# A macaron block on one core: the heads' products in 64-row, 64-column pieces, plain W_v products in the second FFNs, and another order of small steps

## The chip, the cores and the metric

The kernel runs on one core of a Trainium2 chip. The engines of the core work side by side and wait for each other by semaphores: TensorE (PE; its weight loads are shown as PEld), VectorE (DVE), ScalarE (ACT), GpSimd (POOL) and SyncE (SP), which issues most DMAs. The metric is device time in microseconds (us) from start to end of one execution.

## What is computed

The reference, cut to what matters. x has 4096 tokens (2 sequences of 2048) of 256 features; all arithmetic is 32-bit.

```python
def ffn(x):                       # 2 sequences of 2048 tokens, C = 256
    x_prev = x shifted by one token, zeros first
    xr = mu_r * x + (1 - mu_r) * x_prev
    xk = mu_k * x + (1 - mu_k) * x_prev
    r = sigmoid(xr @ W_r.T)
    k_act = square(relu(xk @ W_k.T))
    return r * (k_act @ W_v.T)

def attn(x):                      # 16 heads of 16 features
    q = relu(x @ Wq.T) / 4;  k = relu(x @ Wk.T) / 4
    v = x @ Wv.T;            u = silu(x @ Wu.T)
    kv = einsum('bhlk,bhlv->bhkv', k, v)
    out = einsum('bhlk,bhkv->bhlv', q, kv)
    return (srms_norm(out) * u) @ Wo.T      # norm over the 16 features of a head

x = x + 0.5 * ffn(layernorm(x))
x = x + attn(layernorm(x))
x = x + 0.5 * ffn(layernorm(x))
```

## The kernel before

The tokens are cut into 8 blocks of 512 (NB = 8), each of 4 tiles of 128 tokens. `xs` holds all of x in SBUF from start to end. The program runs through 16 iterations n: n = 0 to 7 are the first FFN of blocks 0 to 7, n = 8 to 15 the second FFN of blocks 0 to 7. Beside the first FFN of block i stand the attention's projections of block i-1 (k, u, q, and the Gram product of x and k, from which kv follows once a sequence is complete), and beside the second FFNs the last steps of the attention of blocks j = n-5. Every engine's stream is written out by hand in program order; nothing is scheduled by a planner. Between the FFN iterations 7 and 8 lies a stretch that has no FFN product, only attention work (blocks 6 and 7).

Most products are "split": the 32-bit operands a and b are cut into a high part, which ACT makes by rounding to the fp32r format, and a low part, the rest, which POOL or DVE makes by subtraction; the product is then three fp32r products, hi*hi, hi*lo and lo*hi (`product`, L1076 to L1079). Other products are "plain": one matmul of 32-bit operands, which the compiler makes into two passes, so that it has two records in the trace. The transposes have one record each.

The steps that the change and the prediction name:

- `attend(j)` (PE, L1234): the heads' outputs of block j. q of the block lies with features on partitions; `kv_bd` is a 128 x 128 matrix for each half of the features, block-diagonal with eight 16 x 16 blocks. For each of 4 token tiles and 2 feature halves one plain product of 128 rows and 128 columns, 16 records a call, 8 calls. They go into two PSUM banks (`psA` for j < 4, `psK` after), tokens of tiles 0 and 1 into the first, 2 and 3 into the second.
- `square_heads` (ACT), `gate_heads` (DVE, L886: times `silu_u`), `head_norms` (DVE, L892 to L921: sum of squares of each head, then a reciprocal root in a chain of 64-element operations, then the first half of gout), `norm_second` (POOL, L265: the second half of gout), `transpose_g` (PE, L1247), `project_out` (PE: split product with Wo), `add_attention` (DVE, L931).
- `ffn_k`, `ffn_r` (PE, split products with W_k and W_r), `transpose_a` (PE, L1094: transposes the normalized block), `previous`, `mix_high` and `normalize` (ACT), `mix_current` (DVE, L806), `k_low` (POOL, L359) and `r_low` (POOL L366 or DVE): they make the mixed inputs of the next FFN and their high and low parts.
- `ffn_v` (PE, split product with W_v, 24 records) and `ffn_v2` (PE, L1146, plain product with W_v, 16 records). The second FFNs n = 8 to 11 use the first, n = 12 to 15 the second: `SPLIT2 = 12` says where it changes. The split one needs `act_hi` (ACT, L565) and `act_lo` (`act_low2`, POOL, L416) beside the square itself (L567).
- `scales_a(n)` (POOL: four small operations on the statistics of `stats_a(n)`, DVE, for the layernorm of FFN n), `scales_b(a)` and `stats_b(a)` (the same for the attention), `add_ffn2(n)` (POOL, L424: adds a second FFN's result to xs, after which SP stores the block), `x1_low`, `kt_low` (POOL, L395 and L404: low parts for the Gram product), `keep_g` (DVE, L871).

Each engine works in its own written order, so a step that waits holds up all that is written behind it on that engine.

## Time and profile before

| | us |
|---|---|
| median of 3 runs | 323.66 (323.63 to 323.96) |
| profiled execution | 323.19 |
| its span, first to last instruction | 321.5 |
| PE busy | 309.6, 96% of the span |
| PE weight loads busy | 280.2, 87% |
| DVE busy | 239.8, 75% |
| ACT busy | 239.7, 75% |
| POOL busy | 215.0, 67% |

An engine's busy time says how full it is. PE's products are pipelined: each record is longer than the distance from its start to the next one's, so a block's price is read from the start of its first record to the start of what follows. The inputs and weights have arrived before a fourth of the span is over; the stores of the second FFNs' blocks run beside the last iterations.

### The profile page before, as it was taken

The page shows a single profiled execution, that of the slowest core. Times are in us where ns is not written, and L with a number is a line of the kernel's source. Part 1 is how long each engine was busy: PE and PEld are TensorE (multiplying, and loading weights), DVE is VectorE, ACT ScalarE, POOL GpSimd, SP SyncE. Part 2 cuts the span into 40 slices and gives each one's busy share as a digit, 9 for nine tenths or more (in the row PEclk, how much of TensorE's full clock was granted, in tenths as well). Part 3 has the DMA queues.
Part 4 walks back from the last instruction along what each step waited for, and adds up shares of the span by engine and source line. Part 5 has one row for each costly group of instructions (what it writes and reads, how often), then busy time and mean ns, then how long its engine had stood idle before and what let it go on. Part 6 is the DMA issues. An engine that isn't in the chain of part 4 may idle for free.

```text
span 321.5 us, 5807 instructions
## 1 busy us (share of the span) xinstructions
PE 309.6 (96%) x2052; PEld 280.2 (87%) x2052; DVE 239.8 (75%) x566; ACT 239.7 (75%) x465; POOL 215.0 (67%) x234
## 2 busy tenths in 40 slices
PE   6898999999999999999999999999999999998996
PEld 6677898899889988988988998889998989887985
DVE  3689984595675746895894797686989988995744
ACT  3698967969869679679259367479797979679861
POOL 4297858769778578669358217536687979797560
PEclk9999999999999999999999999999999999999999
DMA  7960000000000000000000000000002020121103
GB/s 215 352 219 0 3 1 0 2 0 2 0 1 3 0 2 0 0 2 0 2 2 0 2 0 2 0 3 1 2 1 67 0 67 0 66 67 66 65 2 131
DMA packets 11036, 10.85 MB, mean 34 GB/s; under 512 B 768, under 2 KB 11008, under 8 KB 11008
## 3 DMA queue, kind: packets, MB, share of 16 engines
q1 hardware_dynamic: 10432, 10.23, 9.8%
q8 instruction: 16, 0.26, 0.3%
q10 hardware_dynamic: 576, 0.26, 0.3%
q14 instruction: 12, 0.10, 0.1%
HBM read 6.29 MB, written 4.19 MB: 33 GB/s over the span
## 4 chain that ended last, share of the span: by engine, by line
PE 68%; DVE 15%; POOL 7%; issue 5%; ACT 4%; DMA 1%; SPq 0%; POOLq 0%; ACTq 0%
PE psK L1077 7%; PE psK L1078 7%; PE psK L1079 7%; PE psRV L1077 6%; PE psRV L1079 6%; PE psRV L1078 6%; PE psX L1078 6%; PE psX L1077 6%; PE psX L1079 6%; PE psK L1234 2%; PE psA L1094 2%; PE psX L1161 2%; PE psRV L1146 2%; DVE head_ss L892 1%; POOL gout L265 1%
## 5 line engine op out<-in xcount | busy, mean ns | idle before, releaser
L806 DVE SCALAR_TENSOR_TENSOR mix<-psA,mu,mix 128x512 f32<-128x512 f32 x64 | 44.0, 741 | 11.1 <-ACT mix L525 11.1
L359 POOL TENSOR_TENSOR mix_k_lo<-mix,mix_k_hi 128x512 fp32r<-128x512 f32 x30 | 39.2, 1328 | 12.9 <-ACT mix_k_hi L543 12.8
L525 ACT ACTIVATE mix<-psA,one_mu 128x511 f32<-128x511 f32 x64 | 39.5, 696 | 2.2 <-PE psA L1094 2.2
L512 ACT ACTIVATE xn<-xs,shiftA,rstdA 128x256 f32<-128x256 f32 x59 | 30.8, 603 | 12.4 <-POOL shiftA L343 12.4
L1077 PE MATMUL psRV<-ffn_hi,mix_r_hi 128*128 128x256 f32 x128 | 36.4, 284 | 0.0
L1079 PE MATMUL psRV<-ffn_hi,mix_r_lo 128*128 128x256 f32 x128 | 35.8, 279 | 0.0
L1078 PE MATMUL psRV<-ffn_lo,mix_r_hi 128*128 128x256 f32 x128 | 35.7, 279 | 0.0
L1077 PE MATMUL psK<-mix_k_hi,ffn_hi 128*128 128x512 f32 x64 | 26.1, 408 | 1.8 <-DVE mix_k_lo L961 1.5
L1077 PE MATMUL psRV<-ffn_hi,act_hi 128*128 128x256 f32 x96 | 27.5, 287 | 0.0
L1079 PE MATMUL psRV<-ffn_hi,act_lo 128*128 128x256 f32 x96 | 26.8, 279 | 0.0
L1078 PE MATMUL psRV<-ffn_lo,act_hi 128*128 128x256 f32 x96 | 26.8, 279 | 0.0
L1078 PE MATMUL psK<-mix_k_lo,ffn_hi 128*128 128x512 f32 x64 | 25.3, 395 | 0.0
L1079 PE MATMUL psK<-mix_k_hi,ffn_lo 128*128 128x512 f32 x64 | 25.3, 395 | 0.0
L404 POOL TENSOR_TENSOR k_lo<-k_tok,k_hi 128x512 fp32r<-128x512 f32 x14 | 18.1, 1293 | 10.3 <-ACT k_hi L590 10.3
L778 DVE BATCH_NORM_STATS2 statsA<-xs 128x6 f32<-128x256 f32 x64 | 22.6, 412 | 2.7 <-DMA xs<-x_dram 2.4
L1078 PEld LDWEIGHTS psRV<-ffn_lo,mix_r_hi 128*128 128x128 f32 x128 | 24.1, 188 | 0.4
L1077 PEld LDWEIGHTS psRV<-ffn_hi,mix_r_hi 128*128 128x128 f32 x128 | 24.0, 188 | 0.4
L1079 PEld LDWEIGHTS psRV<-ffn_hi,mix_r_lo 128*128 128x128 f32 x128 | 24.0, 188 | 0.0
L543 ACT ACTIVATE mix_k_hi<-mix 128x512 fp32r<-128x512 f32 x32 | 19.9, 653 | 3.5 <-DVE mix L806 3.5
L844 DVE TENSOR_TENSOR x_lo<-psX,x_hi 128x512 fp32r<-128x512 f32 x16 | 10.3, 683 | 14.8 <-ACT x_hi L580 14.7
L333 POOL TENSOR_SCALAR var_epsA<-meanvarA 128x4 f32<-128x4 f32 x16 | 4.7, 294 | 23.7 <-DVE meanvarA L786 22.7
L395 POOL TENSOR_TENSOR x_lo<-xs,x_hi 128x512 fp32r<-128x512 f32 x14 | 17.9, 1302 | 3.5 <-ACT x_hi L585 3.5
(157 smaller groups left out, 1066.3 us busy)
## 6 DMA issues: line engine op xcount, KB each, us to landing
xs<-x_dram SPq DMA_DIRECT2D x7, 512.0 KB, 8.7
out_dram<-xs SPq DMA_DIRECT2D x7, 512.0 KB, 2.9
out_dram<-xs SPq DMA_DIRECT2D x4, 128.0 KB, 1.7
xs<-x_dram ACTq DMA_DIRECT2D x2, 128.0 KB, 2.9
xs<-x_dram SPq DMA_DIRECT2D x2, 128.0 KB, 2.6
silu_u<-w_ffn_k_dram SPq DMA_DIRECT2D x1, 256.0 KB, 5.0
q_store<-w_k_dram SPq DMA_DIRECT2D x1, 256.0 KB, 5.2
silu_u<-w_ffn_r_dram SPq DMA_DIRECT2D x1, 256.0 KB, 6.5
```

The lines of the kernel that those rows point to most:

```text
L359: nc.gpsimd.tensor_tensor(mix_k_lo[:, h, :], mix[:, 0, h, :], mix_k_hi[:, h, :].bitcast(F32), ALU.subtract).then_inc(s_lo_k, 1)
L395: nc.gpsimd.tensor_tensor(x1_lo[:, g * BANK:(g + 1) * BANK], row(xs, a, g * BANK, BANK), x1_hi[:, g * BANK:(g + 1) * BANK].bitcast(F32), A ...
L404: nc.gpsimd.tensor_tensor(k_lo[:, tiles, :], k_tok[:, tiles, :], k_hi[:, tiles, :].bitcast(F32), ALU.subtract).then_inc(s_kt_lo, 1)
L512: nc.scalar.activation(xn[:, t, :], tile_row(xs, b, t), ACT.Identity, bias=shiftA[:, t:t + 1], scale=rstdA[:, t:t + 1]).then_inc(s_xn, 1)
L525: nc.scalar.activation(mix[:, rk, h, 1:BLOCK], psA[:, h, 0:BLOCK - 1], ACT.Copy, scale=one_mu[:, rk, h:h + 1]).then_inc(s_prev, 1)
L543: nc.scalar.activation(hi[:, h, :], mix[:, rk, h, :], ACT.Identity).then_inc(done, 1)
L778: nc.vector.bn_stats(statsA[:, t, :], tile_row(xs, b, t)).then_inc(s_bnA, 1)
L806: nc.vector.scalar_tensor_tensor(out=m, in0=psA[:, h, :], scalar=mu[:, rk, h:h + 1], in1=m, op0=ALU.mult, op1=ALU.add).then_inc(s_mix, 1)
L844: nc.vector.tensor_tensor(x2_lo[:, h, :], psX[:, h, :], x2_hi[:, h, :].bitcast(F32), ALU.subtract).then_inc(s_x2lo, 1)
L1077: nc.tensor.matmul(dst, a_hi, b_hi, start=start, stop=False)
L1078: nc.tensor.matmul(dst, a_hi, b_lo, start=False, stop=False)
L1079: return nc.tensor.matmul(dst, a_lo, b_hi, start=False, stop=stop)
```

## The change

Three things are changed.

1. `attend`: each 128 x 128 product becomes two of 64 rows and 64 columns, for the two 64 x 64 blocks on the diagonal of `kv_bd`; what lies outside them is zero. The products of rows 0 to 63 go into the first PSUM bank and those of rows 64 to 127 into the second, alternating. A bank now holds 64-column pieces of all four token tiles. `gate_heads` and the sum in `head_norms` read the banks in such pieces, and the signals of both banks come with the last two products.
2. W_v of all second FFNs is plain: `ffn_v2` in n = 8 to 11 too. `act_low2` and the ACT operation for `act_hi` are gone there.
3. Order. DVE: `add_attention(0)` and `add_attention(1)` stand ahead of `stats_b(6)` and `stats_b(7)`; `stats_a(9)` stands behind `mix_current(8)`. POOL: `x1_low(7)`, `norm_second(2)`, `kt_low(7)` stand ahead of `scales_a(9)`; from n = 12 on, `add_ffn2(n-1)` stands at the end of the iteration and no longer ahead of `scales_a` and `k_low`.

```diff
+QUAD = 4 * HEAD
-        SPLIT2 = 12
+        def by_quad(ap, g):
+            return ap.rearrange("p (q g e) -> p q g e", g=2, e=QUAD)[:, :, g, :]
...
@@ pool
-            scales_a(9)
-            norm_second(2)
-            x1_low(7)
-            kt_low(7)
+            x1_low(7)
+            norm_second(2)
+            kt_low(7)
+            scales_a(9)
             k_low(8)
             scales_a(10)
             for n in range(8, LAST):
-                if n < SPLIT2:
-                    norm_second(n - 5)
-                    act_low2(n)
-                    if n > 8:
-                        scales_a(n + 2)
-                    k_low(n + 1)
-                    r_low(n + 1)
-                    if n > 8:
-                        add_ffn2(n - 1)
-                else:
-                    if n - 5 < NB:
-                        norm_second(n - 5)
-                    add_ffn2(n - 1)
-                    if n + 2 <= LAST:
-                        scales_a(n + 2)
-                    k_low(n + 1)
-                    if n == 12:
-                        r_low(n + 1)
+                if n - 5 < NB:
+                    norm_second(n - 5)
+                if n > 8 and n + 2 <= LAST:
+                    scales_a(n + 2)
+                k_low(n + 1)
+                if n < 13:
+                    r_low(n + 1)
+                if n > 8:
+                    add_ffn2(n - 1)
             add_ffn2(14)
@@ activate_k2, act
-                        act.wait_ge(s_act_lo, 2 * min(n, SPLIT2))
+                        act.wait_ge(s_act_lo, 2 * NB)
...
-                    if n < SPLIT2:
-                        nc.scalar.activation(act_hi[:, h, :], act_k[:, h, :], ACT.Square).then_inc(s_act_hi, 1)
-                        act.wait_ge(s_act_hi, 2 * n + h + 1)
@@ gate_heads, head_norms, dve
-                    nc.vector.tensor_tensor(gout[:, 2 * g:2 * g + 2, :].rearrange("p t d -> p (t d)"), ps[:, g, :],
-                                            row(silu_u, j % HELD, g * BANK, BANK), ALU.mult).then_inc(s_gu, 1)
+                    nc.vector.tensor_tensor(by_quad(gout[:].rearrange("p t d -> p (t d)"), g),
+                                            ps[:, g, :].rearrange("p (q e) -> p q e", e=QUAD),
+                                            by_quad(row(silu_u, j % HELD), g), ALU.mult).then_inc(s_gu, 1)
...
-                    nc.vector.tensor_reduce(head_ss[:, g * n:(g + 1) * n], by_head(squares[:, g, :]),
+                    nc.vector.tensor_reduce(head_ss[:].rearrange("p (q g k) -> p q g k", g=2, k=4)[:, :, g, :],
+                                            squares[:, g, :].rearrange("p (q k e) -> p q k e", k=4, e=HEAD),
@@ attend, pe
                 for t in range(TILES):
                     for h in range(HALVES):
-                        last = nc.tensor.matmul(ps[:, t // 2, (t % 2) * D + h * P:(t % 2) * D + (h + 1) * P],
-                                                q_half(j, h)[:, tok(t)], kv_bd[:, j // BB, h, :],
-                                                start=True, stop=True)
-                    if t % 2:
-                        last.then_inc(s_o, 1)
+                        for g in range(2):
+                            part = slice(g * QUAD, (g + 1) * QUAD)
+                            col = (t * HALVES + h) * QUAD
+                            last = nc.tensor.matmul(ps[:, g, col:col + QUAD], q_half(j, h)[part, tok(t)],
+                                                    kv_bd[part, j // BB, h, part], start=True, stop=True)
+                            if t == TILES - 1 and h == HALVES - 1:
+                                last.then_inc(s_o, 1)
@@ the second FFNs, pe
                 if n < 12:
                     attend(j + 1, [(s_relu, 2 * (n + 1))])
-                    ffn_v(n)
-                    project_out(j)
-                else:
-                    ffn_v2(n)
-                    project_out(j)
+                ffn_v2(n)
+                project_out(j)
```

DVE's stream between iterations 7 and 8, before, from x2_low(7) to the first silu of block 7 (x_lo<-psX is x2_low(7), statsA and meanvarA are stats_a(9), g_acc is keep_g(6), mix is mix_current(8)):

```order
L844 TENSOR_TENSOR x_lo<-psX,x_hi 128x512 [waits s_x2hi] x2
L778 BN_STATS statsA<-xs 128x6 [waits s_x2,s_aggA]
L778 BN_STATS statsA<-xs 128x6 x3
L786 BN_AGGR meanvarA<-statsA 128x2 [waits s_bnA,s_lnA]
L786 BN_AGGR meanvarA<-statsA 128x2 [waits s_bnA] x3
L871 TENSOR_TENSOR g_acc<-g_acc,psK 128x512 [waits s_gacc,s_gt]
L806 SCALAR_TENSOR_TENSOR mix<-psA,mu,mix 128x512 [waits s_prev] x4
L811 TENSOR_TENSOR halo<-one_mu,psA 128x4
L850 SCALAR_TENSOR_TENSOR silu_u<-psX,rstdB,silu_u 128x256 [waits s_sig] x2
```

And after the change:

```order
L829 TENSOR_TENSOR x_lo<-psX,x_hi 128x512 [waits s_x2hi] x2
L856 TENSOR_TENSOR g_acc<-g_acc,psK 128x512 [waits s_gacc,s_gt]
L791 SCALAR_TENSOR_TENSOR mix<-psA,mu,mix 128x512 [waits s_prev] x4
L796 TENSOR_TENSOR halo<-one_mu,psA 128x4
L763 BN_STATS statsA<-xs 128x6 [waits s_x2,s_aggA]
L763 BN_STATS statsA<-xs 128x6 x3
L771 BN_AGGR meanvarA<-statsA 128x2 [waits s_bnA,s_lnA]
L771 BN_AGGR meanvarA<-statsA 128x2 [waits s_bnA] x3
L835 SCALAR_TENSOR_TENSOR silu_u<-psX,rstdB,silu_u 128x256 [waits s_sig] x2
```

The two rows of statistics and the two of aggregates now follow the four mixes and the halo column.

POOL's stream at the same place, before, from scales_b(7) to k_low(8) (var_epsA to shiftA are scales_a(9), gout is norm_second(2), x_lo<-xs is x1_low(7), k_lo is kt_low(7)):

```order
L352 TENSOR_TENSOR rstd2B<-rstdB 128x4 [waits s_lnB]
L333 TENSOR_SCALAR var_epsA<-meanvarA 128x4 [waits s_aggA]
L339 TENSOR_TENSOR rstdA<-var_epsA,minus_half 128x4 [waits s_xn,s_mvA]
L341 TENSOR_TENSOR mean_rstdA<-meanvarA,rstdA 128x4 [waits s_lnA]
L343 TENSOR_SCALAR shiftA<-mean_rstdA 128x4 [waits s_lnA]
L265 TENSOR_TENSOR gout<-gout,head_rn 128x512 [waits s_gu,s_rn]
L395 TENSOR_TENSOR x_lo<-xs,x_hi 128x512 [waits s_x1hi] x2
L404 TENSOR_TENSOR k_lo<-k_tok,k_hi 128x512 [waits s_kt_hi] x2
L359 TENSOR_TENSOR mix_k_lo<-mix,mix_k_hi 128x512 [waits s_hi_k] x2
```

And after:

```order
L356 TENSOR_TENSOR rstd2B<-rstdB 128x4 [waits s_lnB]
L399 TENSOR_TENSOR x_lo<-xs,x_hi 128x512 [waits s_x1hi] x2
L269 TENSOR_TENSOR gout<-gout,head_rn 128x512 [waits s_gu,s_rn]
L408 TENSOR_TENSOR k_lo<-k_tok,k_hi 128x512 [waits s_kt_hi] x2
L337 TENSOR_SCALAR var_epsA<-meanvarA 128x4 [waits s_aggA]
L343 TENSOR_TENSOR rstdA<-var_epsA,minus_half 128x4 [waits s_xn,s_mvA]
L345 TENSOR_TENSOR mean_rstdA<-meanvarA,rstdA 128x4 [waits s_lnA]
L347 TENSOR_SCALAR shiftA<-mean_rstdA 128x4 [waits s_lnA]
L363 TENSOR_TENSOR mix_k_lo<-mix,mix_k_hi 128x512 [waits s_hi_k] x2
```

scales_a(9), which waits for the aggregates of stats_a(9), went from the head of this piece to behind kt_low(7).

POOL's stream in iterations 12 and 13, before, from norm_second(7) to the add of block 4 (xs<-xs,k_tok is add_ffn2(11), then come scales_a(14), k_low(13), r_low(13), and xs<-xs,gate is add_ffn2(12)):

```order
L265 TENSOR_TENSOR gout<-gout,head_rn 128x512 [waits s_gu,s_rn]
L424 TENSOR_TENSOR xs<-xs,k_tok 128x512 [waits s_gated] x2
L333 TENSOR_SCALAR var_epsA<-meanvarA 128x4 [waits s_aggA]
L339 TENSOR_TENSOR rstdA<-var_epsA,minus_half 128x4 [waits s_xn,s_mvA]
L341 TENSOR_TENSOR mean_rstdA<-meanvarA,rstdA 128x4 [waits s_lnA]
L343 TENSOR_SCALAR shiftA<-mean_rstdA 128x4 [waits s_lnA]
L359 TENSOR_TENSOR mix_k_lo<-mix,mix_k_hi 128x512 [waits s_hi_k] x2
L366 TENSOR_TENSOR mix_r_lo<-mix,mix_r_hi 128x512 [waits s_hi_r] x2
L424 TENSOR_TENSOR xs<-xs,gate 128x512 [waits s_gated] x2
```

And after:

```order
L269 TENSOR_TENSOR gout<-gout,head_rn 128x512 [waits s_gu,s_rn]
L337 TENSOR_SCALAR var_epsA<-meanvarA 128x4 [waits s_aggA]
L343 TENSOR_TENSOR rstdA<-var_epsA,minus_half 128x4 [waits s_xn,s_mvA]
L345 TENSOR_TENSOR mean_rstdA<-meanvarA,rstdA 128x4 [waits s_lnA]
L347 TENSOR_SCALAR shiftA<-mean_rstdA 128x4 [waits s_lnA]
L363 TENSOR_TENSOR mix_k_lo<-mix,mix_k_hi 128x512 [waits s_hi_k] x2
L370 TENSOR_TENSOR mix_r_lo<-mix,mix_r_hi 128x512 [waits s_hi_r] x2
L421 TENSOR_TENSOR xs<-xs,k_tok 128x512 [waits s_gated] x2
```

The add of iteration 11 went behind r_low(13); add_ffn2(12), not shown any more, moved behind k_low(14) in the same way.

## Rows read from the trace of the kernel before

**Rows 1.** The page: busy time, share and instructions of each engine; TensorE's granted clock.

```profile
PE 309.6 (96%) x2052; PEld 280.2 (87%) x2052; DVE 239.8 (75%) x566; ACT 239.7 (75%) x465; POOL 215.0 (67%) x234
...
PEclk9999999999999999999999999999999999999999
```

**Rows 2.** Waits of TensorE: who waited <- for whom: total us, times, longest us.

```profile
PE psRV L1146 <- ACT k_tok L573: 1.1, 1, 1.1
PE psK L1077 <- POOL k_lo L404: 0.7, 1, 0.7
```

**Rows 3.** Timeline of PE in iteration 8: start, length, line, shapes [idle before].

```profile
219.28 1.95 PE L1234 MATMUL psK<-kv_bd,q_store 128*128 128x128 f32 x16
220.98 0.37 PE L1077 MATMUL psRV<-ffn_hi,act_hi 128*128 128x256 f32 x1
...
223.90 0.28 PE L1077 MATMUL psX<-wo_hi,g_hi 128*128 128x256 f32 x1
```

**Rows 4.** Timeline of PE: the plain W_v product of iteration 13 and what follows.

```profile
295.29 3.69 PE L1146 MATMUL psRV<-ffn_v_plain,act_k 128*128 128x256 f32 x16 [1.07 <-ACT k_tok L573]
298.81 1.04 PE L1094 MATMUL psA<-ident,xn 128*128 128x128 f32 x8
```

**Rows 5.** Timeline of PE's weight loads (PEld) behind the wait at 203 us.

```profile
203.12 0.19 PEld L1077 LDWEIGHTS psK<-k_hi,x_hi 128*128 128x128 f32 x1 [0.87 <-POOL k_lo L404]
203.23 0.19 PEld L1078 LDWEIGHTS psK<-k_lo,x_hi 128*128 128x128 f32 x1
```

**Rows 6.** Timeline of PE's products at the same place.

```profile
203.13 0.39 PE L1077 MATMUL psK<-k_hi,x_hi 128*128 128x256 f32 x1 [0.67 <-POOL k_lo L404]
203.35 0.28 PE L1078 MATMUL psK<-k_lo,x_hi 128*128 128x256 f32 x1
```

**Rows 7.** Line 1234, the heads' products: ns shortest/median/longest, first and last start.

```profile
L1234 PE MATMUL psK<-kv_bd,q_store x64: 274/275/276, 219.3 to 267.0; 128*128 128x128 f32 x64
```

**Rows 8.** Timeline of DVE: head_norms in iteration 9 (229) and 10 (243).

```profile
229.09 0.20 DVE L908 TENSOR_SCALAR head_y<-head_ss 128x64 int32<-128x64 int32 x1
...
243.65 0.85 DVE L905 SCALAR_TENSOR_TENSOR head_ss<-var_epsB,head_ss 128x64 f32<-128x64 f32 x1
244.53 1.19 DVE L908 TENSOR_SCALAR head_y<-head_ss 128x64 int32<-128x64 int32 x1
```

**Rows 9.** Timeline of POOL at that time.

```profile
243.14 2.53 POOL L424 TENSOR_TENSOR xs<-xs,gate 128x512 f32<-128x512 f32 x2
```

**Rows 10.** Timeline of PE: both transposes of iterations 10 (247) and 12 (278).

```profile
247.17 1.04 PE L1094 MATMUL psA<-ident,xn 128*128 128x128 f32 x8
248.42 0.63 PE L1247 MATMUL psX<-ident,gout 128*128 128x128 f32 x4 [0.21 <-DVE gout L265]
249.25 0.66 PE L1247 MATMUL psX<-ident,gout 128*128 128x128 f32 x4 [0.20 <-POOL gout L265]
...
278.65 1.03 PE L1094 MATMUL psA<-ident,xn 128*128 128x128 f32 x8
279.53 0.60 PE L1247 MATMUL psX<-ident,gout 128*128 128x128 f32 x4
280.32 0.66 PE L1247 MATMUL psX<-ident,gout 128*128 128x128 f32 x4 [0.20 <-POOL gout L265]
```

**Rows 11.** Timeline of POOL, iterations 12 and 13: the add of block 3 and r_low(13).

```profile
280.23 2.50 POOL L424 TENSOR_TENSOR xs<-xs,k_tok 128x512 f32<-128x512 f32 x2
...
287.24 2.52 POOL L366 TENSOR_TENSOR mix_r_lo<-mix,mix_r_hi 128x512 fp32r<-128x512 f32 x2
```

**Rows 12.** Timeline of ACT there: mix_high(13, 0), second half, and previous(14).

```profile
284.12 0.63 ACT L543 ACTIVATE mix_k_hi<-mix 128x512 fp32r<-128x512 f32 x1 [0.57 <-DVE mix L806]
...
289.84 0.21 ACT L519 ACTIVATE mix<-halo 128x4 f32<-128x4 f32 x1 [2.08 <-issue]
```

**Rows 13.** Timeline of DVE between iterations 7 and 8: stats_a(9) and keep_g(6).

```profile
192.87 1.39 DVE L778 BATCH_NORM_STATS2 statsA<-xs 128x6 f32<-128x256 f32 x4
...
194.47 0.65 DVE L871 TENSOR_TENSOR g_acc<-g_acc,psK 128x512 f32<-128x512 f32 x1
```

More of the change, by code:

```diff
@@ L410, in norm_second @@
                 norm_half(nc.gpsimd, 1).then_inc(s_gn1, 1)
-            def act_low2(n):
-                for h in range(HALVES):
-                    pool.wait_ge(s_act, 2 * (n - NB) + h + 1)
-                    nc.gpsimd.tensor_tensor(act_lo[:, h, :], act_k[:, h, :], act_hi[:, h, :].bitcast(F32),
-                                            ALU.subtract).then_inc(s_act_lo, 1)
             def add_ffn2(n):
@@ L885, in gate_heads @@
                         dve.wait_ge(s_tg, 2 * j)
-                    nc.vector.tensor_tensor(gout[:, 2 * g:2 * g + 2, :].rearrange("p t d -> p (t d)"), ps[:, g, :],
-                                            row(silu_u, j % HELD, g * BANK, BANK), ALU.mult).then_inc(s_gu, 1)
+                    nc.vector.tensor_tensor(by_quad(gout[:].rearrange("p t d -> p (t d)"), g),
+                                            ps[:, g, :].rearrange("p (q e) -> p q e", e=QUAD),
+                                            by_quad(row(silu_u, j % HELD), g), ALU.mult).then_inc(s_gu, 1)
             def head_norms(j):
-                n = heads // 2
                 for g in range(2):
-                    nc.vector.tensor_reduce(head_ss[:, g * n:(g + 1) * n], by_head(squares[:, g, :]),
+                    nc.vector.tensor_reduce(head_ss[:].rearrange("p (q g k) -> p q g k", g=2, k=4)[:, :, g, :],
+                                            squares[:, g, :].rearrange("p (q k e) -> p q k e", k=4, e=HEAD),
                                             AX_X, ALU.add).then_inc(s_ss, 1)
@@ L1009, in _ @@
                 add_ffn1(i, 1)
+                if i == 6:
+                    add_attention(0)
                 stats_b(i)
@@ L1015, in _ @@
                 if i == 6:
-                    add_attention(0)
                     stats_a(8)
@@ L1027, in _ @@
                 add_ffn1(7, g)
+            add_attention(1)
             stats_b(7)
-            add_attention(1)
             gate_heads(2)
@@ L1032, in _ @@
             x2_low(7)
-            stats_a(9)
             keep_g(6)
             mix_current(8)
+            stats_a(9)
             projections(7)
```

## The prediction, made before the changed kernel was run

> **What bounds the kernel now.** I read the page first, for which engine is full; then the waits of TensorE (PE), for what is left to win on it; then PE's timeline block by block, for the price of each kind of product; last VectorE (DVE), GpSimd (POOL) and ScalarE (ACT) at the three places where PE does wait. On the page PE is busy 96% of the span and the granted clock is at its full level, 2.4 GHz, in every slice [rows 1]. "Busy" overlaps for pipelined products, so the check is the waits: beyond the first 35 us PE's longest are 1.1 us for ACT before the W_v product of iteration 13 and 0.7 us for POOL's k_lo before the last Gram product [rows 2]. So nearly everything that lengthens PE's stream lengthens the kernel, and what ACT and POOL are relieved of counts only at the few places where PE waits. I price every edit on PE first.
>
> **W_v plain in iterations 8 to 11.** Before: 24 split products, from 220.98 to 223.90, 2.92 us [rows 3]. Plain: 16 passes, from 295.29 to 298.81, 3.52 us [rows 4]. That is +0.60 us four times, +2.4 us. POOL loses 8 subtractions and ACT 8 squares; PE does not wait for either in these iterations, so this gives nothing by itself.
>
> Part of the 2.4 is swallowed. In iterations 10, 11 and 12 PE waits inside or ahead of the transposes of gout. Eight transposes ahead take 0.88 us (278.65 to 279.53), 0.11 each; four take 0.79 in iteration 12, so 0.35 of that is waiting, and in iteration 10 it is 1.25-0.88 = 0.37 plus 0.83-0.44 = 0.39 [rows 10]. Iteration 11 has one such wait like iteration 12's, 0.38. What ends late is the chain project_out, add_attention, head_norms on DVE, then gout on POOL. In it two 64-element operations take 0.85 and 1.19 us where one of them takes 0.20 in iteration 9 [rows 8]; they end with the two halves of POOL's add, which runs from 243.14 for 2.53 us [rows 9]. That add comes where it does because of r_low and k_low ahead of it, and those follow ACT, which follows the transposes and not W_v. So if project_out ends 0.6 us later, DVE arrives 0.6 us later at an obstacle that lifts at the same time, and the transposes are ready as before: the extra 0.6 us of the iteration before is hidden as far as there was waiting: 0.6 in iteration 10, 0.38 in 11, 0.35 in 12, -1.3 us together. If the add moves with project_out, this cover is gone and 1.3 us come back; if without act_low2 POOL gets to the add early, DVE is blocked less and it is some tenths better. I take -1.3.
>
> **Heads' products.** Eight calls. Before, each is 8 products, 16 passes of 128 rows and 128 columns, 219.28 to 220.98 and on to the first full-length record behind it, 1.7 to 1.8 us: 0.11 a pass [rows 3]. After: 32 passes of 64 rows and 64 columns. Two things are needed for each pass, the 128-column load of q and the streaming. Streaming is proportional to columns (a plain 256-column pass 3.52/16 = 0.22, a 128-column one 0.11) [rows 3, 4], so 64 columns want 0.055. The load is the question. Steady rows hide it. After the stall at 203 they don't: the second load starts 0.11 us behind the first (203.12, 203.23), and the first product behind the stall takes 0.39 against 0.28, 0.11 more [rows 5, 6]. So a plain load of 128 columns occupies its path for 0.11 us, and a pass was bound by both equally. The load still has 128 columns (tokens). If the two row halves load at the same time, each half does 16 loads of 0.11 = 1.76 us, which is what stands there now; halving the streaming gives nothing. The bounds: with loads that cost half for half the rows, 16 x 0.055 = 0.88, -0.9 a call; with loads one after another, 32 x 0.11 = 3.52, +1.76 a call. Any emptying of the array between the two shapes adds at most what a product's record is longer than its distance, 0.275-0.11 = 0.165 [rows 7], twice, 0.33. No row shows two row halves at work, so the value is a choice: 1.76, the one nearest to the measured load, 0 us.
>
> The Trainium skill (TensorE: Matmul & The Clock Gate, the section on packing small matmuls) says that an LDWEIGHTS overlaps a running matmul only when the row group differs. The trace disagrees for full-height products: load and product overlap there on the same rows, or a split pass could not come every 0.12 us with a 0.11 us load and 0.11 us of streaming. By that rule the change would win; by the row there is no such gain left to take.
>
> The signal for the first half of the heads now comes with the last product and not 0.9 us earlier. In iteration 7 that delays DVE by some 0.3 us, and the next product that needs DVE there has about as much room. The gating and the sum over heads are the same elements in 64-column pieces; I take 0. Were the sum in the chain above twice as long, it would be +1.2 us in three iterations; that is in the upper end of the range.
>
> **New order between iterations 7 and 8.** PE waits 0.7 us for k_lo [rows 2, 6]. stats_a(9), 192.87 to 194.47, 1.6 us of DVE [rows 13], goes behind mix_current(8), so ACT's mix_high(8, 0) and with it sigmoid_u(7) and kt_high(7) start up to 1.6 us earlier; on POOL x1_low(7), norm_second(2) and kt_low(7) no longer queue behind scales_a(9), which waits for those statistics. What is late next is the last result of k_and_u itself, and by my count k_lo is then ready 0.5 us ahead of PE. -0.7 us. scales_a(9) itself comes later by some 7 us, and is needed only by normalize(9) after q_of(7). The moved add_attention(0) and (1) delay stats_b(6), (7) and r_low(7) by 1.2 us, with POOL idle behind them.
>
> **New order on POOL from iteration 12 on.** The add of block 3 (280.23, 2.50 us) went ahead of scales_a(14), k_low(13) and r_low(13), which ends at 289.76 [rows 11]; ACT's previous(14) waits for that r_low and starts at 289.84 [rows 12], ahead of activate_k2(13), for which PE waits 1.1 us [rows 2, 4]. With the add behind r_low, POOL is free 2.5 us earlier and k_low(13) then waits for ACT instead: its second half for mix_k_hi, which ends at 284.12+0.63 = 284.75 [rows 12]. Behind that stand one half of k_low, 1.3, and both of r_low, 2.5 [rows 11]: 288.6, 1.1 us earlier. The transposes that previous(14) also needs are done by then. -1.1 us (0.5 to 1.2). The adds end 5 to 8 us later, before the sigmoids that wait for them (those of iteration n wait for the add of n-2) with about 2 us in hand; the stores behind them are under the last products. In iteration 14 the late wait is for ACT's mix_k_hi, not for the add: 0.
>
> **Sum.** The profiled execution took 323.19 us: its span 321.5 and 1.7 around it. +2.4 -1.3 +0 -0.7 -1.1 = -0.7: 322.5. The median of the runs is 323.66, 0.47 above that execution, so 323.0 is the forecast for the median.
>
> **Rivals.**
> 1. The heads' products do halve (chance 0.22): a half-height load costs half, or several loads are in flight. For: nothing in the trace; against: the 0.11 us load, set by columns that stay 128. Price: first four calls -0.9 each = -3.6, with 0.4 of the k_lo wait coming back; iteration 8 +0.6-0.9 = -0.3; in iterations 9 to 11 the DVE and POOL chain holds the pace and neither the -0.3 nor the -1.3 is had; order -0.7-1.1. Together -5.3: 318.4.
> 2. Loads run one after another (0.18, the case on the other side): one load path for both row halves. Place: every attend; price 32 x 0.11 - 1.76 = +1.76 a call, 14.1 in eight; it decides as soon as a pair of loads takes over 0.11 us together, that is a call over 1.85 us. For: loads in all rows follow each other at 0.11 or more. Against: all of those use all rows. -0.7+14.1: 337.0.
> 3. The array empties at each change of shape (0.12): 0.33 a call from [rows 7], 2.6 us in all. -0.7+2.6: 325.6. The trace has no change of row count to show it; changes between plain and split products cost nothing there. The Trainium skill (TensorEngine Tiling (Array Packing), Key Properties) states such a drain at each change of tiling mode; there is one into and one out of every call.
>
> **How the numbers follow.** Forecast case 0.48, rivals 0.22, 0.18, 0.12. The own range of the forecast case is 321.5 to 325 (the 1.3 of cover lost, or small gains in the blocked chain). The range is 316.5 to 327.5: it holds the first and third rival and leaves out the second. A measurement of this kernel can tell 0.2%, 0.65 us, from no change. The forecast case lies on that edge: 0.24 faster, 0.14 same, 0.10 slower; rival 1 is faster; rival 2 slower; rival 3 0.08 slower and 0.04 same. So faster 0.46, same 0.18, slower 0.36.
>
> **What would show it.** In the new profile: a heads' call of 1.7 to 1.9 us (0.9: rival 1; 2.1: rival 3; 3.5: rival 2); W_v blocks of 3.5 us in iterations 8 to 11; no wait of PE for k_lo near 202 and less than 0.3 us before W_v of iteration 13; waits at the gout transposes of iterations 10 to 12 gone or under 0.1. I am wrong if the heads' call is anything but 1.7 to 1.9, or if those waits stay although W_v is longer.

## The result, and the profile after

The changed kernel is slower: 325.50 us in the median of 4 runs (325.17 to 325.87) against 323.64 for the kernel before in the same session (323.63 to 323.96). The ratio is 1.0065, with an interval of 1.0048 to 1.0083, so the forecast of 323.0 missed its size and its sign. The time is inside the range, and within 0.1 us of what the third rival gave (325.6). The profiled execution took 325.17 us, its span 323.4, against 323.19 and 321.5: +2.0 us.

The page of the changed kernel, to be read against [rows 1]:

```profile
PE 313.4 (97%) x2148; PEld 281.4 (87%) x2148; DVE 240.4 (74%) x566; ACT 235.7 (73%) x457; POOL 206.0 (64%) x226
...
PEclk9999999999999999999999999999999999999999
```

ACT lost 4.0 us of work and POOL 9.0, as the diff says, and the kernel got longer all the same: what grew is PE, from 309.6 to 313.4. The granted clock is at its full level, 2.4 GHz, in both, so the clock is no part of the answer.

Of the waits of PE (who waited <- for whom: total us, times, longest), to be read against [rows 2], the one that is new:

```profile
PE psX L1064 <- DVE xs L917: 0.7, 1, 0.7
```

Both waits of [rows 2] are gone, and so are the four for gout and the 0.2 us for mix_k_lo. This row is new: a product waits 0.7 us for `xs` of L917, which is add_attention(2). The only other waits (2.6, 1.5, 1.2 and 0.5 us in all) stand in the kernel before too, with the same times.

PE in iteration 8 (timeline: start, length, engine, line, shapes), against [rows 3]:

```profile
218.32 1.03 PE L1081 MATMUL psA<-ident,xn 128*128 128x128 f32 x8
219.20 1.04 PE L1237 MATMUL psX<-ident,gout 128*128 128x128 f32 x8
220.16 2.00 PE L1225 MATMUL psK<-kv_bd,q_store 64*128 64x64 f32 x32
222.09 3.72 PE L1133 MATMUL psRV<-ffn_v_plain,act_k 128*128 128x256 f32 x16
225.46 0.47 PE L1064 MATMUL psX<-wo_hi,g_hi 128*128 128x256 f32 x1
```

Eight transposes that run on into further transposes take 0.88 us (218.32 to 219.20). Eight that run into the heads' call take 0.96 (219.20 to 220.16): 0.09 is lost on the way into the call. The call takes 1.93 us from its first product to the first behind it, where [rows 3] have 1.70.

The weight loads (PEld) of the same call, in two narrow stretches, the first pair and a later one:

```profile
220.16 0.19 PEld L1225 LDWEIGHTS psK<-kv_bd,q_store 64*128 64x128 f32 x2 [0.17 <-issue]
...
220.27 0.30 PEld L1225 LDWEIGHTS psK<-kv_bd,q_store 64*128 64x128 f32 x4
```

Two loads fill 0.19 us together and four fill 0.30, where a single load's record is 0.18 long: the loads of the two row halves start together (in the single records 7 ns apart) and one pair follows the other at 0.11. The assumption on which the prediction put its value of 1.76 us is what happens. The added 0.3 us per call is at the two ends: in the single records the first product behind the transposes comes 0.20 us after the last of them, the second pair of products 0.16 us after the first, and the W_v product 0.20 us after the last pair (221.89 to 222.09), where a step in between is 0.11.

The end of the chain into iteration 13, with the W_v product of [rows 4] and what follows it:

```profile
296.95 3.69 PE L1133 MATMUL psRV<-ffn_v_plain,act_k 128*128 128x256 f32 x16
300.48 1.27 PE L1081 MATMUL psA<-ident,xn 128*128 128x128 f32 x8
301.50 0.48 PE L1064 MATMUL psK<-mix_k_hi,ffn_hi 128*128 128x512 f32 x1
```

The wait of 1.07 us ahead of W_v is gone. The transposes behind it take 1.02 us, where the kernel before has 0.80 at this place (298.81 to 299.61). What removed the wait is seen in POOL's r_low(13), to be read against [rows 11], and PE at the transposes of iteration 12:

```profile
288.90 2.52 POOL L370 TENSOR_TENSOR mix_r_lo<-mix,mix_r_hi 128x512 fp32r<-128x512 f32 x2
```

```profile
281.54 1.04 PE L1081 MATMUL psA<-ident,xn 128*128 128x128 f32 x8
```

Beside the kernel before, PE is 2.89 us late at these transposes (278.65 to 281.54) and POOL only 1.66 at r_low(13) (287.24 to 288.90): it ends 1.2 us earlier by PE's clock.

Iteration 12 at the gout transposes, against [rows 10]:

```profile
282.42 1.10 PE L1237 MATMUL psX<-ident,gout 128*128 128x128 f32 x8
283.35 1.03 PE L1133 MATMUL psRV<-ffn_v_plain,act_k 128*128 128x256 f32 x4
```

Eight transposes in one group, 0.93 us against 0.88 without any wait: the 0.35 is covered down to 0.05. Some of it comes back one step later: the transposes of iteration 13, which wait for ACT in both kernels, take 1.51 us (289.63 to 291.14) and took 1.24 before.

### The profile page after: what moved, and what is told of

It is laid out like the page before. It is cut to its first block, busy times and chain, and to the rows that moved or that the text cites. A ratio compares the mean times of both kernels' runs of the same rounds, so it can differ in the third digit from the quotient of the medians.

```text
span 323.4 us, 5983 instructions
## 1 busy us (share of the span) xinstructions
PE 313.4 (97%) x2148; PEld 281.4 (87%) x2148; DVE 240.4 (74%) x566; ACT 235.7 (73%) x457; POOL 206.0 (64%) x226
## 4 chain that ended last, share of the span: by engine, by line
PE 84%; DVE 6%; POOL 3%; ACT 2%; issue 2%; DMA 1%; SPq 0%; POOLq 0%; ACTq 0%
PE psK L1064 8%; PE psK L1065 8%; PE psK L1066 8%; PE psRV L1133 7%; PE psX L1064 7%; PE psRV L1066 6%; PE psRV L1065 6%; PE psRV L1064 6%; PE psX L1065 6%; PE psX L1066 6%; PE psA L1081 3%; PE psK L1225 2%; PE psA L1225 2%; PE psX L1148 2%; PE psX L1237 2%
## 5 line engine op out<-in xcount | busy, mean ns | idle before, releaser
L1133 PE MATMUL psRV<-ffn_v_plain,act_k 128*128 128x256 f32 x120 | 27.9, 384 | 0.0
L1133 PEld LDWEIGHTS psRV<-ffn_v_plain,act_k 128*128 128x128 f32 x120 | 22.2, 190 | 3.2
L811 DVE TENSOR_TENSOR mix_r_lo<-mix,mix_r_hi 128x512 fp32r<-128x512 f32 x20 | 16.0, 838 | 6.5 <-ACT mix_r_hi L531 6.5
L269 POOL TENSOR_TENSOR gout<-gout,head_rn 128x512 f32<-128x512 f32 x8 | 12.0, 1496 | 12.9 <-DVE head_rn L907 12.9
```

What stands on the lines that cost most here:

```text
L1133: last = nc.tensor.matmul(dst, act_k[:, c, tok(t)], ffn_v_plain[:, c, :], start=(c == 0), stop=(c == HALVES - 1))
```

## The experiments

The expectations speak of theory D: PE loses a gap each time it goes from products that use 128 rows to products that use 64, and back. Its main rivals are that the half-height passes themselves are slower than 0.11 us, and that the loss comes from the other two parts of the change. The ratios are to the kernel before, run on the same chip beside them: 322.85, 322.96 and 322.95 us in the three sessions. The forecasts up to the second session count from 323.65 us for the kernel before and 325.5 for the changed one. The kernel before ran 0.7 to 0.8 us faster than that here, so they are to be compared by ratio or difference and not by the bare time.

### Which part costs what

**The changed kernel with the old heads' products** (`attend`, `gate_heads` and `head_norms` as before):

```diff
-                        for g in range(2):
-                            last = nc.tensor.matmul(ps[:, g, col:col + QUAD], q_half(j, h)[part, tok(t)], ...)
+                        last = nc.tensor.matmul(ps[:, t // 2, ...], q_half(j, h)[:, tok(t)], kv_bd[:, j // BB, h, :], ...)
```

> The changed kernel with the heads' products of before (128 x 128, a bank for two token tiles) and its readers on VectorE; plain W_v and the new order stay. Theory D (the array empties and its loads lie bare at each change between 128-row and 64-row work, 0.34 us a call, 2.7 us in eight): 325.5 - 2.7 = 322.8, or up to 323.3 if some of the waits that the later stream covered come back. Rival W (the plain W_v products are the loss, not hidden anywhere, and the heads' form costs under 0.5 us): 325.0 or more.

Measured: 323.35 us, ratio 1.0013 (1.0002 to 1.0024). Taking the new heads' products out brings most of the loss back, 1.7 to 2.3 us of it (the changed kernel has 1.0065, and 1.0085 when run again below). That is less than theory D forecast: 322.8 to 323.3 would be ratios of 0.997 to 0.999. PE in iteration 8 of this kernel:

```profile
218.05 1.04 PE L1233 MATMUL psX<-ident,gout 128*128 128x128 f32 x8
218.92 1.95 PE L1220 MATMUL psK<-kv_bd,q_store 128*128 128x128 f32 x16
220.71 3.62 PE L1132 MATMUL psRV<-ffn_v_plain,act_k 128*128 128x256 f32 x16
223.98 0.47 PE L1063 MATMUL psX<-wo_hi,g_hi 128*128 128x256 f32 x1
```

Into the call 0.87 us, not 0.96; the call 1.79, not 1.93; from the first W_v product to project_out 3.27, not 3.37, because the first load behind half-height products is not hidden: the first two W_v products start 0.32 us apart there (222.09 and 222.41) and 0.22 here (220.71 and 220.93). 0.09+0.14+0.10: from the transposes to project_out it is 5.93 us here and 6.26 with the new products, +0.33. Iterations 9 to 11 have 5.05 to 5.06 us from call to project_out here and 5.30 there. Of the 2.6 us for eight calls, 0.3 us goes into a longer wait for add_attention(2) (1.03 for 0.71) and 0.5 us into waits at the gout transposes of iterations 10 to 12 that come back. The readers on DVE are no part of it: the sum over the heads takes 0.677 us and the gating 0.682 in the changed kernel, 0.676 and 0.68 in the kernel before.

**The kernel before with the new heads' products alone:**

```diff
-                        last = nc.tensor.matmul(ps[:, t // 2, ...], q_half(j, h)[:, tok(t)], kv_bd[:, j // BB, h, :], ...)
+                        for g in range(2):
+                            last = nc.tensor.matmul(ps[:, g, col:col + QUAD], q_half(j, h)[part, tok(t)], ...)
```

> The kernel before with the new heads' products and their readers alone. Theory D: 0.34 us a call; the four of the first FFNs lie bare, of the four of the second up to three are covered by waits for gout: 323.65 + 1.7 to 2.7 = 325.3 to 326.4. Rival W: 323.7 to 324.2.

Measured: 324.40 us, ratio 1.0048 (1.0036 to 1.0061): +1.55 us, less than the +1.7 to +2.7 that was forecast and than 8 x 0.33 = 2.6. The trace says where 0.9 us of the missing 1 us went. The last call of the kernel before, and then of this one:

```profile
265.29 1.95 PE L1234 MATMUL psK<-kv_bd,q_store 128*128 128x128 f32 x16
267.27 0.39 PE L1077 MATMUL psRV<-ffn_hi,act_hi 128*128 128x256 f32 x1
```

```profile
265.71 2.00 PE L1244 MATMUL psK<-kv_bd,q_store 64*128 64x64 f32 x32
267.64 0.39 PE L1083 MATMUL psRV<-ffn_hi,act_hi 128*128 128x256 f32 x1
```

The old call takes 1.98 us here, not 1.70: the split W_v behind it waits 0.28 us for its operand `act_lo`, which POOL ends at 267.22 us, and the profile does not list so short a wait. Under the longer call it disappears, so that in iterations 10 and 11 the call costs only the entry. Another 0.33 went under the first gout wait of iteration 10. Where W_v is plain it does not wait for that operand, so in the changed kernel this cover is not there.

**W_v alone plain in iterations 8 to 11, in the kernel before:**

```diff
-                    ffn_v(n)
+                    ffn_v2(n)
...
-                    act_low2(n)
```

The ACT operation for act_hi is gone too.

> The kernel before with plain W_v in iterations 8 to 11 alone. PE blocks +0.63 us four times = 2.5 us. With the cover forecast in the prediction (longer blocks eat the waits for gout in iterations 10 to 12) +1.2: 324.9. Without any cover +2.5: 326.2. If the relief of ScalarE and GpSimd is worth more than the waits seen: under 324.3.

Measured: 324.02 us, ratio 1.0033 (1.0021 to 1.0044): +1.06 us. The prediction had +2.4-1.3 = +1.1 for this part. In the trace iterations 8 and 9 get 0.63 us longer, iterations 10 and 11 only 0.33 to 0.35, since there the split products had that wait of 0.28 us ahead of them: the blocks cost about +1.9, not +2.4. PE at the gout transposes of iteration 10 in this kernel:

```profile
248.53 1.22 PE L1243 MATMUL psX<-ident,gout 128*128 128x128 f32 x8
249.59 1.95 PE L1230 MATMUL psK<-kv_bd,q_store 128*128 128x128 f32 x16
```

1.06 us against 1.32 in [rows 10] (248.42 to 249.74), with 0.18 of waiting left and none ahead of them: the cover is smaller too, 1.0 us in iterations 10 to 12. The two errors are in opposite directions.

**The changed kernel with W_v split again in these iterations:**

```diff
-                ffn_v2(n)
+                    ffn_v(n)
...
+                    act_low2(n)
```

> The changed kernel with W_v of iterations 8 to 11 split again (act_hi on ScalarE, act_lo on GpSimd behind norm_second); the new heads' products and the new order stay. Theory D: the PE blocks get 4 x 0.63 = 2.5 us shorter, but the waits for gout that they covered come back up to 1.3, so 323.0 to 324.5, still no faster than before. Rival W: 323.0 or less, since the whole loss is W_v.

Measured: 323.88 us, ratio 1.0034 (1.0022 to 1.0047), which is 1.0 to 1.6 us less than the changed kernel. Rival W, by which the whole loss was W_v, forecast 323.0 or less, a ratio under 0.998, and is out; theory D's forecast goes up to 1.003.

**The new order alone, in the kernel before** (the third part of the change, with act_low2 kept at its place; add_attention(0) and (1) are moved too, which is not shown):

```diff
-            stats_a(9)
             keep_g(6)
             mix_current(8)
+            stats_a(9)
...
-            scales_a(9)
-            norm_second(2)
             x1_low(7)
+            norm_second(2)
             kt_low(7)
+            scales_a(9)
...
-                    add_ffn2(n - 1)
                     k_low(n + 1)
                     if n == 12:
                         r_low(n + 1)
+                    add_ffn2(n - 1)
```

> The kernel before with the new order on VectorE and GpSimd alone. By the trace after, the wait for k_lo (0.8 us) goes but one of 0.9 us for add_attention(2) takes its place, and the wait ahead of W_v in iteration 13 (1.2 us) goes against 0.4 us that come at the transposes: 323.65 - 0.8 = 322.9 (322.4 to 323.4). Rival O (the order itself is a loss, since GpSimd's later work blocks VectorE): 323.8 to 325.

Measured: 322.21 us, ratio 0.9981 (0.9969 to 0.9994): -0.6 us, where the prediction had -1.8. The three parts one by one give +1.55+1.06-0.64 = +2.0 us, and the whole change measured +1.9 in its own session (+2.6 in a later one, below). They add up within the intervals, which are about 0.4 us to either side for each part; they need not do so exactly, since the heads' products and the plain W_v hide under the same waits.

### Why the order gives so little

Both waits that it was to remove are gone, but PE waits at a new place. The waits of PE in the kernel with the order alone:

```profile
PE psX L1078 <- DVE xs L931: 1.0, 1, 1.0
```

DVE at that time in the same kernel, and in the kernel before:

```profile
204.59 2.43 DVE L826 TENSOR_TENSOR mix_r_lo<-mix,mix_r_hi 128x512 fp32r<-128x512 f32 x2
206.94 1.27 DVE L931 TENSOR_TENSOR xs<-xs,psX 128x512 f32<-128x512 f32 x2
```

```profile
205.45 1.28 DVE L826 TENSOR_TENSOR mix_r_lo<-mix,mix_r_hi 128x512 fp32r<-128x512 f32 x2
206.99 0.69 DVE L931 TENSOR_TENSOR xs<-xs,psX 128x512 f32<-128x512 f32 x1 [0.26 <-PE psX L1079]
208.41 0.69 DVE L931 TENSOR_TENSOR xs<-xs,psX 128x512 f32<-128x512 f32 x1 [0.72 <-PE psX L1079]
```

Before, DVE's r_low(8) took 1.28 us and was done ahead of PE: the add waited for PE. With the new order the same two operations take 2.43 us, and the add starts late. What they meet is on POOL; the changed kernel's own timeline of it:

```profile
204.56 2.55 POOL L363 TENSOR_TENSOR mix_k_lo<-mix,mix_k_hi 128x512 fp32r<-128x512 f32 x2
```

`scales_a(9)`, now behind kt_low(7), holds k_low(8) back until 204.56, and k_low(8) then runs beside r_low(8) (206.17, 2.09 us in the changed kernel). POOL's pair takes the same 2.5 us beside it as alone; r_low(8) is what gets longer, by 0.81 us where the last 0.94 us of POOL's pair stand beside it, and with the order alone by 1.15 us where the last 1.28 us do (204.59 to 205.87). The Trainium skill (SBUF — State Buffer, "SBUF: two separate sides") says that a VectorE operation with two SBUF inputs and a GpSimd operation that reads SBUF exclude each other. The 2.43 against 1.28 us here agrees. The test is one line: the add ahead of r_low(8) on DVE.

```diff
-            r_low(8)
             add_attention(2)
+            r_low(8)
```

In the changed kernel:

> The changed kernel with add_attention(2) ahead of r_low(8) on VectorE. Theory: the wait of 0.9 us for add_attention(2) comes from r_low(8), which runs beside GpSimd's mix_k_lo and takes 2.1 us in place of 1.3; with the add first it is ready when project_out(2) ends and the wait goes: 324.6 to 324.8. Rival: the add is late because project_out's second half is late, then 325.5 as before.

Measured: 324.68 us, ratio 1.0049 (1.0030 to 1.0068), against 1.0065 and 1.0085 for the changed kernel. The intervals of 1.0049 and 1.0065 overlap, so the trace decides here: the wait is gone from the list of PE's waits, and PE is 0.87 us earlier behind it. And in the kernel with the order alone, which is the version that the experiments point to:

> The kernel before with the new order alone, and add_attention(2) ahead of r_low(8): heads' products and W_v as before. Order alone measured 0.998 of before, and its trace has a wait of 1.2 us for add_attention(2); with that gone 0.9945 (321.1 where before is 322.9). If the add is held up by something else than r_low(8): 0.998.

Measured: 320.82 us, ratio 0.9940 (0.9923 to 0.9957), 2.1 us less than the kernel before and 4.7 less than the changed one run beside it; the order without this line had 0.9981, and these two intervals do not meet. DVE in this kernel:

```profile
205.53 0.69 DVE L931 TENSOR_TENSOR xs<-xs,psX 128x512 f32<-128x512 f32 x1 [0.59 <-PE psX L1080]
206.95 0.69 DVE L931 TENSOR_TENSOR xs<-xs,psX 128x512 f32<-128x512 f32 x1 [0.72 <-PE psX L1080]
207.55 1.29 DVE L826 TENSOR_TENSOR mix_r_lo<-mix,mix_r_hi 128x512 fp32r<-128x512 f32 x2
```

DVE waits for PE again and not PE for DVE, and r_low(8), which comes later than POOL's pair, takes 1.29 us. With this line the order is worth the -1.8 that the prediction gave it: -2.1 in the medians, and -1.8 in the traces behind the first 30 us. The full-height variant of the next section says the same without the moved line: its longer calls let POOL's pair end at 211.24, r_low(8) starts at 211.67 and takes 1.28 us, and PE does not wait for the add.

### What a half-height product costs

**All 128 rows, but 64 columns** (32 passes; the other half of the rows multiplies zeros):

```diff
-                            last = nc.tensor.matmul(ps[:, g, col:col + QUAD], q_half(j, h)[part, tok(t)],
-                                                    kv_bd[part, j // BB, h, part], start=True, stop=True)
+                            last = nc.tensor.matmul(ps[:, g, col:col + QUAD], q_half(j, h)[:, tok(t)],
+                                                    kv_bd[:, j // BB, h, part], start=True, stop=True)
```

> The changed kernel with the heads' products of 64 columns but all 128 rows: same banks, same output, twice the weight loads of before and no change of height. If a pass is bound by its 128-column weight load (0.11 us) and full-height loads can't be side by side: 32 x 0.11 = 3.5 us a call and no gap at its ends, 325.5 - 2.7 + 8 x 1.76 = 336.9. If a pass is bound by streaming (64 columns, 0.055): 1.76 us a call, 322.8.

Measured: 335.65 us, ratio 1.0396 (1.0376 to 1.0416), where the forecast of 336.9 would be 1.041. PE in iteration 8:

```profile
223.90 1.04 PE L1237 MATMUL psX<-ident,gout 128*128 128x128 f32 x8
224.77 3.68 PE L1225 MATMUL psK<-kv_bd,q_store 128*128 128x64 f32 x32
228.29 1.95 PE L1133 MATMUL psRV<-ffn_v_plain,act_k 128*128 128x256 f32 x8
```

3.52 us for 32 passes is 0.11 each with half the columns: the load sets the pass, the streaming doesn't. And the way into the call is 0.87 us: no gap without a change of height, though the columns, the banks and the readers are those of the changed kernel.

**The half-height products of rows 0 to 63 first, then those of rows 64 to 127:**

```diff
+                for g in range(2):
                     for t in range(TILES):
                         for h in range(HALVES):
-                        for g in range(2):
...
```

> The changed kernel with its 64-row products in another order: all 8 of rows 0 to 63, then all 8 of rows 64 to 127, so that neighbours are on the same half. If the loads of the two halves run side by side only when neighbours alternate: 3.5 us a call and the same gaps at the ends, 325.5 + 8 x 1.7 = 338 to 339. If the queue reaches further ahead than the next pair, or one half's loads are faster than 0.11 us: less, down to 325.5.

Measured: 338.42 us, ratio 1.0455 (1.0422 to 1.0489). A call at full clock:

```profile
228.43 3.39 PE L1225 MATMUL psK<-kv_bd,q_store 64*128 64x64 f32 x32
231.75 0.48 PE L1133 MATMUL psRV<-ffn_v_plain,act_k 128*128 128x256 f32 x1
```

3.32 us for 32 passes, 0.104 each: half the rows do not make a load shorter to speak of (the passes of one half follow each other at 0.11; only at the turn do some of both halves run side by side). Two halves at work at once is all that the new form has over this one, and that only brings it back to the time of the old. So rival 1 had nothing to draw on, and rival 2 describes this variant and not the changed kernel. A call is 1.39 us longer than in the changed kernel, not the forecast 1.7: 11.1 us in eight. That the time came out as forecast is luck, since the rest has another cause, told under the last heading.

**One more product of full height in each call, ahead of all others or between its halves.** Both kernels do the same added work (two passes of 128 rows and 64 columns a call, of which the result is overwritten), but in the second it adds two changes of height:

```diff
                 for t in range(TILES):
+                    if t == 0:        # in the other kernel: t == 2
+                        nc.tensor.matmul(ps[:, 0, 3 * P:3 * P + QUAD], q_half(j, 0)[:, tok(0)],
+                                         kv_bd[:, j // BB, 0, 0:QUAD], start=True, stop=True)
```

> The changed kernel with one more plain product of 128 rows and 64 columns at the head of each heads' call; its result is written over by the products behind it. It stands next to other full-height work, so it costs its two passes alone: 8 x 0.22 = 1.8 us over the changed kernel, 1.0115 of before or a little less where it eats a wait. No theory says more.

> The same additional product in the middle of each heads' call, between the 64-row products of tiles 1 and 2. Theory D (every change of height empties the array): two more changes a call, 8 x (0.22 + 0.34) = 4.5 us over the changed kernel, 2.7 over the one with the product at the start. Rival: the gaps at the ends of a call come from what stands there (a wait for a semaphore, another bank), not from the change of height: the same time as with the product at the start, within 0.5 us.

With them the changed kernel ran again:

> The changed kernel itself, beside the next three on the same chip: 1.005 to 1.008 of the kernel before, as the sum of its three parts measured alone (heads +1.55, plain W_v +1.06, order -0.6 us: +2.0 us, 1.006).

Measured: the changed kernel 325.55 us (ratio 1.0085, 1.0065 to 1.0105), the product at the start 326.38 (1.0105, 1.0086 to 1.0124), in the middle 328.36 (1.0174, 1.0154 to 1.0194). PE at the start variant, then the middle one:

```profile
220.00 1.04 PE L1241 MATMUL psX<-ident,gout 128*128 128x128 f32 x8
220.87 0.33 PE L1223 MATMUL psK<-kv_bd,q_store 128*128 128x64 f32 x2
221.13 2.00 PE L1229 MATMUL psK<-kv_bd,q_store 64*128 64x64 f32 x32
223.06 2.21 PE L1133 MATMUL psRV<-ffn_v_plain,act_k 128*128 128x256 f32 x9
```

```profile
220.42 1.04 PE L1241 MATMUL psX<-ident,gout 128*128 128x128 f32 x8
221.39 1.11 PE L1229 MATMUL psK<-kv_bd,q_store 64*128 64x64 f32 x16
222.43 0.43 PE L1223 MATMUL psK<-kv_bd,q_store 128*128 128x64 f32 x2
222.79 1.11 PE L1229 MATMUL psK<-kv_bd,q_store 64*128 64x64 f32 x16
223.83 1.35 PE L1133 MATMUL psRV<-ffn_v_plain,act_k 128*128 128x256 f32 x5
```

With the product at the start there is no gap between the transposes and the call (220.00 to 220.87 is 0.87 again); the height changes behind it. From the transposes to W_v is 3.06 us there and 3.41 with the product in the middle, against 2.89 in the changed kernel (219.20 to 222.09). The same work costs 0.17 us at one place and 0.52 at the other; the difference, 0.35, is one pair of changes. Eight of them are 2.8 us. In the traces 2.5 us of that show from 60 us on, since PE's wait for add_attention(2) gives way by 0.34. The medians differ by 1.98 only. The profiled execution of the second kernel has a start that is 0.9 us shorter, which fits, but the runs show no cause for it. The first variant's 0.83 us fell short of its forecast of 1.8: the added passes take part of the gap, 0.17 a call in place of 0.22, and the wait for the add gives way by 0.2.

## Why the prediction was wrong, step by step

**Heads' products (+0): the step that failed.** Its first half held: 16 pairs of loads at 0.11 us, both halves at once. What failed is the last bound of that step, the emptying of the array "between the two shapes", which the prediction had sized at 0.33 us a call from [rows 7] and then set to 0 because nothing in the trace spoke for it. The trace of before had no change of row count in it, so its silence was no evidence. The size of the bound is what was measured: 0.33 us a call by the kernel with the old heads' products, 0.35 between the two variants with an added product. This is the rule of the Trainium skill (TensorEngine Tiling (Array Packing), Key Properties) that was cited with rival 3: the traces agree, with a price that they alone supply. They show the gap and that it comes with the change of height, not what the array does in it. Some of the cost hides under waits, so that all eight calls cost 1.55 us in the kernel before and 1.7 to 2.3 in the changed one. That the cost comes out at the bound is not shown to be more than a coincidence: it is not twice 0.165 but 0.09 ahead of the call, 0.14 in it and 0.10 behind it. In the step's own test, 1.93 us is more than the 1.7 to 1.9 of the forecast and less than the 2.1 of rival 3. A test that reads the call alone misses more than half of the cost. Nor did it tell rival 2, for which the prediction had set a limit of 1.85 us: the pairs of loads still take 0.11 together.

**W_v plain (+2.4-1.3 = +1.1): right in the net, not in its parts.** Alone it gave +1.06 us, from about +1.9 for the blocks and 1.0 of cover. The size of one block, +0.60, is close to the 0.63 us measured in iterations 8 and 9, but partly by luck: the 3.52 us were read from iteration 13 alone, and the same trace has 3.27 in iteration 12 (280.81 to 284.08). In iteration 8 the kernel with the old heads' products has 3.27 as well, and the rest stands ahead of the block (1.79 for 1.70) and behind it, in project_out (3.01 for 2.82). So the blocks of 3.5 us that the prediction named as a sign did not come; in the changed kernel they are 3.37. In the whole change the cover is there as predicted: the gout waits of iterations 10 to 12 are gone or under 0.1 us. That the obstacle on DVE and POOL lifts at the same time as before was not tested by itself.

**Order, k_lo (-0.7): the wait went, the gain did not come.** The prediction looked at what is late next for the same product, and found 0.5 us of room. It did not look at what the moved `scales_a(9)` pushes behind it. It is a step of its own queue, ahead of k_low(8), so the argument that it "is needed only by normalize(9)" left out the instruction behind it on POOL. That one now runs beside DVE's r_low(8) and keeps it from the add for which PE waits next. The two kernels with the add first show it.

**Order, POOL from iteration 12 (-1.1): right for the wait, too high for what it is worth.** The wait ahead of W_v of iteration 13 fell from 1.07 to about 0.1 us, and the 1.2 us at r_low(13) are the step's 1.1. Right behind W_v 0.22 us come back, in the transposes (1.02 for 0.80), and ahead of it 0.27 at the transposes of iteration 13. From W_v of iteration 12 to the end PE gains 0.65 us, with the order alone 0.9.

**Sum.** Predicted +2.4-1.3+0-0.7-1.1 = -0.7 for the profiled execution; measured +2.0 for it, +1.9 for PE's stream, a difference of 2.6. How much later PE is than in the kernel before, stretch by stretch:

| PE's stream | predicted | measured |
|---|---|---|
| start of the kernel, to 33 us | 0 | -0.5 |
| to the last Gram product at 202 us, with four heads' calls | 0 | +1.3 |
| the wait for k_lo | -0.7 | -0.9 |
| the new wait for the add | 0 | +1.0 |
| iterations 8 to 11, to W_v of iteration 12 | +2.4-1.3 | +1.7 |
| from there to the end | -1.1 | -0.65 |

In iterations 8 to 11 four calls (4 x 0.33) and four W_v blocks (4 x 0.63) are 3.8 us; 2.1 of it is hidden, 1.5 under the gout waits and 0.55 where the split W_v had waited for act_lo. The start is no part of the change as far as the runs show: the transposes at 30 us start anywhere from 29.0 to 30.2 us in the traces. Without it the stream is 2.4 us longer, between the 1.9 of the first measurement and the 2.6 of the second. That rival 3's time, 325.6, was met within 0.1 us is luck in part: its sum has all 2.6 us of the heads' calls and 1.8 us gained by the order, and the runs have less of both.

## What to carry to other kernels

Where a product is split into products of fewer rows, first see whether its pass is set by the load or by the columns. Here the load sets it, two halves at once bring back what the split took and no more, and each pair of changes between full and half height costs 0.33 to 0.35 us on top, so a call of 1.8 us loses. A mechanism of which the trace of before has no example must not be set to nothing because the trace is silent; it goes into the sum at its bound or the middle of it. Where an instruction is moved back in an in-order queue, look not only at who needs its result but at what it now delays behind it, and at what that meets on the neighbouring engine: one line more, the add ahead of r_low(8), made the new order worth 2.1 us in place of 0.6.

## What the runs showed of the hardware

Two half-height loads of different row halves start 7 ns apart (the changed kernel, from 220.16 us on) and share a slot of 0.11 us. A change of height and back costs 0.33 to 0.35 us.

The kernel with the halves in turn also lost clock. Its page has this row for the granted clock:

```profile
PEclk9999999999999999599999999999979999999999
```

The window from 137 to 139 us of it (us, busy time of PE, PEld, DVE, ACT and POOL, granted clock, DMA share, GB/s):

```profile
137.00:139.00 2.00, 2.00 (x8) 1.69 (x8) 0.85 (x2) 1.03 (x2) 0.17 (x1) 0.50 0.00 0
```

And PE's timeline from the first call on:

```profile
134.10 3.83 PE L1225 MATMUL psA<-kv_bd,q_store 64*128 64x64 f32 x32
137.86 0.79 PE L1064 MATMUL psX<-x_hi,att_hi 128*128 128x512 f32 x1
138.45 0.63 PE L1065 MATMUL psX<-x_lo,att_hi 128*128 128x512 f32 x1
138.88 0.63 PE L1066 MATMUL psX<-x_hi,att_lo 128*128 128x512 f32 x1
```

The products behind the call follow each other at 0.43 us where they follow at 0.23 otherwise, and the clock in the window is 0.50: TensorE is at its 1.2 GHz level there. It fell at 136.9 us, in the second half of this call, and was back at 143.7. It fell a second time at 249.5 us, 0.6 us behind the end of another call (245.60 to 248.92), and was back at 252.9. The two stretches lengthened PE's stream by 3.1 and 1.7 us beyond what the calls themselves did. In the four executions of this kernel the mean granted clock was 0.984 to 0.995, and the one with 0.995 was the fastest, 336.09 us against 340.27. Behind the other calls of the same form the clock did not fall, and it fell in the trace of none of the other kernels, in which no call works on one half of the rows for long. Why only two of eight calls did it stays open.
